# Causal attention with a softmax whose future is cleared by GpSimd: that engine's scaling, bias and additions placed in other score steps

## What is computed

```python
h = _layernorm(x) * (1 + ca) + sa                  # "x": scaled by GpSimd
att = softmax(where(causal, q @ k.T / 4, -inf))    # 16 heads, 1024 x 1024
x = x + ga * ((att @ v) @ Wp + bp)                 # bias and additions by GpSimd
h = _layernorm(x) * (1 + cb) + sb                  # "f": scaled by GpSimd
x = x + gb * ffn(h)                                # two more layers, not touched here
```

## Time and profile before

| | |
|---|---|
| median of 3 runs | 4243.48 us (4224.47 to 4245.86) |
| the profiled execution | 4219.14 us, of which the program's span is 4217.4 us |
| attention stage in it | about 0 to 1512 us, the two layers behind it 1512 to 4217 us |
| TensorE busy over the span | 3790.9 us, 90% |
| GpSimd busy over the span | 2105.5 us, 50% |

### The profile page before, as it was taken

How to read it: one execution, slowest core, us unless ns; L and a number is a source line. 1 busy time by engine, 2 the same in 40 slices (tenths; PEclk the granted TensorE clock), 3 DMA queues, 4 the chain that set the end, 5 groups by cost and what they waited for, 6 DMA issues and landing times.

```text
span 4217.4 us, 84635 instructions
## 1 busy us (share of the span) xinstructions
PE 3790.9 (90%) x31022; PEld 2881.4 (68%) x31022; DVE 3088.6 (73%) x7229; ACT 2613.4 (62%) x5759; POOL 2105.5 (50%) x2082
## 2 busy tenths in 40 slices
PE   4888898888988748999999999999999999999997
PEld 2344545444444337888888888888888888888886
DVE  5677666766677447778777787778788788888884
ACT  1455445544555426777777777777777777777774
POOL 1244444434444324555555555555565666656664
PEclk6889879978899769999999999999999999999998
DMA  5334243442443011000000000011000000000000
GB/s 130 86 66 123 59 100 74 90 121 61 100 98 77 25 61 37 17 17 19 15 20 17 17 19 16 19 35 44 29 26 22 26 23 28 26 23 25 23 24 21
DMA packets 146009, 195.72 MB, mean 46 GB/s; under 512 B 21596, under 2 KB 119608, under 8 KB 145600
## 3 DMA queue, kind: packets, MB, share of 16 engines
q1 hardware_dynamic: 145600, 190.31, 18.0%
HBM read 113.66 MB, written 67.16 MB: 43 GB/s over the span
## 4 chain that ended last, share of the span: by engine, by line
PE 24%; DVE 14%; ACT 12%; DMA 8%; issue 5%; POOL 1%; DVEq 0%; POOLq 0%; SPq 0%; ACTq 0%
PE b_bank_m L1948 10%; DMA b_hs<-b_fr 7%; PE b_bank_p L1948 5%; ACT b_e L1828 4%; DVE b_e L2176 3%; PE b_bank_et L2013 2%; DVE b_qk_rot L2145 2%; PE b_bank_t L1948 2%; ACT L1871 2%; DVE b_rot L2149 2%; PE b_bank_ot L2028 2%; PE b_bank_s L2002 1%; ACT b_e_t L1838 1%; DVE b_ag L2240 1%; ACT b_ag L1863 1%
## 5 line engine op out<-in xcount | busy, mean ns | idle before, releaser
L763 ACT ACTIVATE a_e_t<-a_ring 128x1024 f32<-128x1024 f32 (+3 forms) x768 | 610.6, 809 | 585.1 <-PE a_ring L941 580.2
L1084 DVE TENSOR_REDUCE a_mx<-a_ring 128x2 f32<-128x1024 f32 (+3 forms) x768 | 724.3, 956 | 274.7 <-PE a_ring L904 130.8
L1716 POOL TENSOR_TENSOR b_e<-b_e,b_share 128x512 f32<-128x512 f32 (+1 forms) x512 | 506.0, 991 | 802.8 <-DVE b_share L2184 802.6
L1828 ACT ACTIVATE b_e<-b_e,b_bias 128x256 f32<-128x256 f32 (+1 forms) x1024 | 494.4, 487 | 163.9 <-DVE b_bias L2176 162.8
L664 POOL TENSOR_SCALAR_AFFINE_SELECT a_e_t<-a_e_t 128x256 f32<-128x256 f32 x512 | 205.4, 407 | 720.6 <-ACT a_e_t L763 717.5
L2176 DVE CUSTOM_DVE_ANT_0 b_e<-b_bank_s,b_mask,b_inv 128x256 f32<-128x256 f32 (+1 forms) x1024 | 415.6, 460 | 33.3 <-PE b_bank_s L2002 33.3
L1701 POOL TENSOR_TENSOR b_qk_rot<-b_qk_rot,b_rot 128x512 f32<-128x512 f32 x256 | 352.4, 1386 | 129.8 <-DVE b_rot L2149 129.8
L941 PE MATMUL a_ring<-a_q_st,a_k_st 50*128 50x512 f32 (+3 forms) x1536 | 364.5, 474 | 49.5 <-DVE a_mx L1084 21.2
L1838 ACT ACTIVATE b_e_t<-b_bank_et 128x512 f32<-128x512 f32 (+1 forms) x512 | 287.3, 561 | 184.4 <-PE b_bank_et L2013 184.3
L917 PE MATMUL a_ring<-a_k_st,a_q_st 48*128 48x512 f32 (+3 forms) x1536 | 323.7, 419 | 83.5 <-ACT a_e_t L763 48.3
L958 PE MATMUL a_outp<-a_e_t,a_v_t 128*32 128x512 f32 (+3 forms) x3072 | 370.3, 557 | 30.5 <-POOL a_e_t L664 17.9
(11 more groups left out here) (235 smaller groups left out, 11117.4 us busy)
## 6 DMA issues: line engine op xcount, KB each, us to landing
a_q_st<-a_parts_q SPq DMA_DIRECT2D x192, 128.0 KB, 4.7
a_k_st<-a_parts_k SPq DMA_DIRECT2D x192, 128.0 KB, 7.5
a_parts_q<-a_qk_p SPq DMA_DIRECT2D x16, 1024.0 KB, 7.7
a_parts_k<-a_qk_p SPq DMA_DIRECT2D x16, 1024.0 KB, 9.6
b_fl<-f_rows SPq DMA_DIRECT2D x64, 256.0 KB, 4.2
a_xl<-in_L_attn_x SPq DMA_DIRECT2D x9, 1024.0 KB, 5.2
a_x<-in_L_attn_x SPq DMA_DIRECT2D x8, 1024.0 KB, 9.1
x_rows<-a_x SPq DMA_DIRECT2D x8, 1024.0 KB, 4.6
```

The costliest lines, as they stand in the source:

```text
L763: act.activation(e_t[:, step % 2, 2 * pair:2 * pair + 2, 0:cols], slot[:, :].rearrange("p (h t) -> p h t", h=2)[:, :, 0:cols], ACT.Exp).th ...
L1084: dve.reduce_max(mx[:, g % 2, :, pair, piece, t:t + 1], slot[:, :].rearrange("p (r c) -> p r c", r=2)[:, :, 0:cols], AX.X)\
L1716: pool.tensor_tensor(weights, weights, share[:, h % SPS, 2 * j:2 * j + 2].unsqueeze(2) .broadcast_to([P, 2, 2 * WIN - lo]), ALU.mult).then ...
L1828: ins = act.activation(weights, weights, ACT.Exp, scale=-1.0, bias=bias[:, h % SPS, at:at + 1], accum_out=total[:, h % SPS, at:at + 1])
```

## The change

The three tables become four, keyed by (group, step), and GpSimd's loop looks each of them up. In numbers of pieces per step:

| work | before | after |
|---|---|---|
| `modulate_f` | (1, 1) to (1, 3) one each, (1, 4) to (1, 7) two each, (1, 8) to (1, 10) one each, (1, 11) two | (1, 0) to (1, 3) one each, (1, 4) to (1, 7) three each |
| `add_bias` | (2, 8) to (2, 11) one each | (2, 5) one, (2, 6) one, (2, 7) two |
| `modulate_x` | as `modulate_f`, in group 3 | (3, 4) to (3, 6) three each, (3, 7) two, (0, 2) one, (0, 4) and (0, 5) two each |
| `add_rows` | (0, 6) two, (0, 8) two | (0, 6) two, (0, 8) one, (0, 9) one |

```diff
-PIECES_AT = (0, 1, 1, 1, 2, 2, 2, 2, 1, 1, 1, 2)
-BIAS_AT = ((2, 8), (2, 9), (2, 10), (2, 11))
-ROWS_AT = ((0, 6), (0, 8))
+F_AT = {(1, n): k for n, k in enumerate((1, 1, 1, 1, 3, 3, 3, 3))}
+X_AT = {(3, 4): 3, (3, 5): 3, (3, 6): 3, (3, 7): 2, (0, 2): 1, (0, 4): 2, (0, 5): 2}
+BIAS_AT = {(2, 5): (0,), (2, 6): (1,), (2, 7): (2, 3)}
+ROWS_AT = {(0, 6): (0, 1), (0, 8): (2,), (0, 9): (3,)}
...
+def pieces_at(plan, at):
+    place = lambda at: ((at[0] - 1) % G1, at[1])
+    before = sum(k for other, k in plan.items() if place(other) < place(at))
+    return range(before, before + plan.get(at, 0))
...
-            def add_rows(p, i):
+            def add_rows(q, i):
                 pool.wait_ge(biased.sem, biased.at(i, 1))
-                pool.wait_ge(gated.sem, gated.at(i, 2 * p + 2))
-                for q in range(2):
-                    ts = slice(4 * p + 2 * q, 4 * p + 2 * q + 2)
-                    ins = pool.tensor_tensor(x1[:, ts, :], x1[:, ts, :], f_t[:, ts, :], ALU.add)
-                ins.then_inc(x1_done.sem, 1)
+                pool.wait_ge(gated.sem, gated.at(i, 2 * (q // 2) + 2))
+                ts = slice(2 * q, 2 * q + 2)
+                ins = pool.tensor_tensor(x1[:, ts, :], x1[:, ts, :], f_t[:, ts, :], ALU.add)
+                if q % 2:
+                    ins.then_inc(x1_done.sem, 1)
```

More of the change, by code:

```diff
@@ L265 @@
 SCALED = 12
-PIECES_AT = (0, 1, 1, 1, 2, 2, 2, 2, 1, 1, 1, 2)
-BIAS_AT = ((2, 8), (2, 9), (2, 10), (2, 11))
-ROWS_AT = ((0, 6), (0, 8))
-assert sum(PIECES_AT) == SCALE_PIECES and len(PIECES_AT) == NSTEP
+F_AT = {(1, n): k for n, k in enumerate((1, 1, 1, 1, 3, 3, 3, 3))}
+X_AT = {(3, 4): 3, (3, 5): 3, (3, 6): 3, (3, 7): 2, (0, 2): 1, (0, 4): 2, (0, 5): 2}
+BIAS_AT = {(2, 5): (0,), (2, 6): (1,), (2, 7): (2, 3)}
+ROWS_AT = {(0, 6): (0, 1), (0, 8): (2,), (0, 9): (3,)}
+assert sum(F_AT.values()) == sum(X_AT.values()) == SCALE_PIECES
+def pieces_at(plan, at):
+    place = lambda at: ((at[0] - 1) % G1, at[1])
+    before = sum(k for other, k in plan.items() if place(other) < place(at))
+    return range(before, before + plan.get(at, 0))
 UNIT_AT = ((5, 1), (3, 0), (2, 0), (0, 0), (5, 0), (4, 0), (1, 0), (4, 1), (7, 1), (7, 0), (6, 1), (6, 0))
@@ L694, in program @@
                             clear_future(g, n, a)
-                        before = sum(PIECES_AT[:n])
-                        for k in range(before, before + PIECES_AT[n]):
-                            if g == 1 and i > 0:
+                        if i > 0:
+                            for k in pieces_at(F_AT, (g, n)):
                                 modulate_f(k, i - 1)
-                            if g == 3 and mode == "body":
+                        if mode != "lead":
+                            for q in BIAS_AT.get((g, n), ()):
+                                add_bias(q, i)
+                        if mode == "body":
+                            for k in pieces_at(X_AT, (g, n)):
                                 modulate_x(k, i + 2)
-                        if (g, n) in BIAS_AT:
-                            add_bias(BIAS_AT.index((g, n)), i)
-                        if mode == "body" and (g, n) in ROWS_AT:
-                            add_rows(ROWS_AT.index((g, n)), i)
+                            for q in ROWS_AT.get((g, n), ()):
+                                add_rows(q, i)
                 if mode == "closing":
-                    add_rows(0, i)
+                    for q in range(2):
+                        add_rows(q, i)
                     rows, shape = f_t[:, END:TB, :], [P, TB - END, C]
```

## The result

| | before | with the change |
|---|---|---|
| median, timed side by side | 4237.73 us (4 runs, 4224.47 to 4245.86) | 4187.27 us (4 runs, 4183.47 to 4198.07) |
| the profiled execution | 4219.1 us | 4189.7 us |
| its span, and mean granted clock | 4217.4 us, 0.938 | 4187.9 us, 0.945 |

The ratio is 0.9888, 95% interval 0.9854 to 0.9922: 1.1% faster.

The account below looks back on a forecast made before the run. In the attention stage GpSimd was not the bound, only the moment of its clearings, for which TensorE waited 17.9 us. Direct 5.2 plus clock 6.3 gave 11.5 us off the 4243.5 median: 4232 us, range 4208 to 4254.

Parts of the forecast that it names:

- The direct gain: Attention stage: shorter TensorE waits for clearings, 4.2 us from the `f` pieces and 1.0 from row additions, 5.2 in all.
- The bias: Group 2: addition runs once `x1` has landed, done 5.5 us before GpSimd is next needed; costed at nothing.
- The `x` pieces and the row additions: Groups 3 and 0: eleven `x` pieces fit with 0.9 us to spare, gaining nothing; row additions gain 1 us in all.
- The clock: Group 2: denser TensorE work avoids one clock fall in four, 6.3 us, between none and a bound of 29 us.
- the wait is not the whole cause, but it stands right where the clock falls: Group 2, wait at (2, 0): denser work there should keep the clock up more often; 6.3 us taken.
- The text named that case as one that would prove it wrong: Groups 3 or 0 changing their granted clock more than group 2 would show the prediction wrong.
- The sign that the prediction had set for its clock term: Group 2: fewer than four of the six bodies with `f` pieces lose clock.
- waits as short as those here would not matter: By the skill's rule on TensorE's idle gaps, no clock would come back in group 2, leaving the direct 5 us.
- Most of the clock comes back: Rival: three or more falls in group 2 avoided, 20 to 31 us, 4218 us in the middle; chance 0.2.

Follow-up runs that it names:

- x_only: The kernel before with only the table of the `x` pieces as changed: 4232.43 us, ratio 0.9994.
- rows_only: The kernel before with only the row additions split over (0, 8) and (0, 9): 4232.98 us, ratio 0.9991.
- f_only: The kernel before with only the table of the `f` pieces as changed: 4188.51 us, ratio 0.9888.
- bias_only: The kernel before with only the bias table as changed: 4219.42 us, ratio 0.9969.
- The filled kernels: Unread TensorE transposes added ahead of the values of (g, 0): four in group 2 of before, 0.9920; in every group of before, 0.9909, or changed, 0.9836.
- A second filling: Four more unread transposes in step (g, 0), added to the changed kernel that already had four in (g, 1): 4209.61 us, ratio 0.9945 to before.

## Why the prediction was wrong

**The direct gain.** Right in place and nearly in size. The waits on the clearings fell from 17.9 to 11.7 us, with 4.2 predicted for the waits and 5.2 in all, and at (2, 0) ScalarE's copy is what ends a wait that is left. The 0.70 us was not the wait of every body: those of before with the pair had 0.23 to 0.83 us. Another direct part was missed: seven times 1.05 us of VectorE's held instruction, an upper bound of 7.4 us.

**The bias.** "Nothing" was worked out for GpSimd's side, and that side held. SyncE issues the load of `x1` 3.6 us after the start of (2, 0), as predicted (it was 7.7), and the bias ends with 6.3 us to spare before GpSimd's next clearing waits for ScalarE:

```profile
895.19 0.43 SPq L558 DMA_DIRECT2D a_x<-in_L_attn_x  x1
...
903.54 0.73 POOL L680 TENSOR_TENSOR a_gate_bp<-a_modb,a_b_p 128x256 f32<-128x256 f32 x1 [0.86 <-DMA a_x<-in_L_attn_x]
904.35 4.98 POOL L683 TENSOR_TENSOR a_x<-a_x,a_gate_bp 128x512 f32<-128x512 f32 x4
915.64 0.41 POOL L672 TENSOR_SCALAR_AFFINE_SELECT a_e_t<-a_e_t 128x256 f32<-128x256 f32 x1 [6.32 <-ACT a_e_t L773]
```

The step that failed is that I asked only when the addition would run, not what ran beside it on VectorE in its old place. The Trainium skill has the rule on the page "SBUF — State Buffer", section on the two separate sides: VectorE's instructions with two SBUF inputs and GpSimd's share a port pair under an exclusive lock, and the one that comes second is blocked for the whole instruction. I had weighed the short form of this rule only as a thing that might slow GpSimd. The trace agrees with the page in the other direction: VectorE's instruction took 1.22 us beside an addition, in all seven bodies, and 0.17 alone.

**The `x` pieces and the row additions.** Right: x_only and rows_only are at 0.9994 and 0.9991. The run of eleven pieces ends 0.83 us before the next clearing needs GpSimd, with 0.9 predicted:

```profile
1264.27 9.66 POOL L646 TENSOR_SCALAR a_xl<-a_xl,a_x_aggr,a_x_rstd 128x256 f32<-128x256 f32 x8
1274.01 3.76 POOL L650 TENSOR_TENSOR a_xl<-a_xl,a_mod_in 128x512 f32<-128x512 f32 x3
1278.61 0.41 POOL L672 TENSOR_SCALAR_AFFINE_SELECT a_e_t<-a_e_t 128x256 f32<-128x256 f32 x1 [0.83 <-ACT a_e_t L773]
```

**The clock.** This is the term that failed, by size and by reach: 6.3 us for one fall of four avoided in group 2. Over the 95 runs of the eleven kernels without filling, time follows the mean granted clock with a correlation of -0.99, 2.8 us for each 0.001, and a scatter of 3 us around the line. The runs of the changed kernel stand at 0.944 to 0.949. A line through the 29 runs of before beside the first experiments (2.7 us per 0.001) gives 4198 us at their mean of 0.9465, and they took 4189. The line is carried past the highest clock of those 29 runs, 0.942, so what follows is an estimate: about 9 of the 50 us are direct and about 40 are clock. Most of it is what the pair does, since putting the pair back loses 38 of 47 us. The reading in the prediction was "the wait is not the whole cause, but it stands right where the clock falls", and from that I took a value near none. The runs put in its place: the clock falls in (2, 1) with or without the pair, and the pair makes the difference between a fall of 3.4 us and one of 34 or more: 15 of 15 such falls were long with it, and 3 of 16 where it was moved away. Two bodies of before had the wait and kept the clock, and I took that for evidence against a large gain; but the wait costs clock only in those bodies where the clock has just fallen. Nor was the wait alike where the clock was lost for long: it was 0.63 us in one of the two bodies and 0.23 in the other. I had also bounded the term by group 2 alone, at 29 us. The trace showed group 3 at five low lengths out of seven before, and I left them out because the direct gain hardly touches group 3. The text named that case as one that would prove it wrong, if group 3 changed more than group 2. It changed nearly as much, 24.0 against 25.6 us, and its mean granted clock rose from 0.828 to 0.942, that of group 2 from 0.856 to 0.985. With f_only, which leaves the bias, group 3 fell by 20 us too, and with bias_only, which leaves the pair, by 29. So neither move alone accounts for it, and whether a clock that is held in one group helps the next is not settled here. The sign that the prediction had set for its clock term, fewer than four of the six bodies losing clock in group 2, did come: only the fourth body lost any.

One reading of the earlier trace rows was off as well, with no weight in the sum: the first 15 slices go down to six tenths, and the last of the 40 stands at eight.

The Trainium skill's rule on falls (page "TensorE: Matmul & The Clock Gate", section on HAM oscillation) puts them down to idle gaps of TensorE between bursts. The prediction read it as saying that "waits as short as those here would not matter". The filled kernels agree with its kind, since more work of TensorE kept the low stretches short, and the traces contradict that reading: 0.63 us of idle time went with a low stretch of 34 us. Three other long ones had no wait in front of the values, so idle time is not the whole of it.

**The rivals.** "Most of the clock comes back" was the right one in kind; its 4218 was still too high by 31 us, since it counted group 2 alone. The nearest row to have used was the first body, the only one without the pair: its group 2 had kept the clock, and I called one body little.

**What stays open.** What makes the clock fall in (2, 1), in (3, 0) to (3, 3) and in the closing part in the first place was not isolated. Nor was what it is in TensorE's work behind the fall in (2, 1) that decides its length. A second filling loses in two ways: beside the line through the runs of before, its runs lie 21 us above and those with one filling 5 above, so by this estimate some 16 of the 40 us are there at equal clock and the rest is clock; why the clock is lost is open. Each kernel was profiled once, so the counts of bodies come from one execution each.

## What to carry to other kernels

Where the time of many runs follows the mean granted clock, look at what TensorE does just behind a fall of the clock, short idle times among it, and not only for the longest waits: here the pair of pieces that caused 0.2 to 0.8 us of waiting there was worth 38 us. Useless matmuls in such a wait are a quick test of whether it is the clock, and sometimes a gain that stays. And when side work is placed in GpSimd's gaps, look at what VectorE does at the same moment, not only at whether GpSimd is free.

## What the hardware did that I had not expected

- A low stretch of the clock that begins 0.2 to 1.3 us into (2, 1) lasted 3.4 us (25 times) or 34.1 to 37.5 us (18 times), and never anything between. In the kernels without filling, less than 0.1 us in the start of one group of matmuls parts the latest of the short ones (0.82 us behind the fall) from the earliest of the long ones (0.89).
- Four useless transposes, 0.66 us at full clock and 1.11 at the lower one, in each group but the lead-in's, made the changed kernel some 20 us faster; with eight it was 40 us slower than with four.
- A VectorE instruction of 128 x 8 numbers takes 0.17 us alone, 0.32 to 0.34 beside a clearing of 0.41 us and 1.22 beside an addition of 1.28 us. GpSimd's own durations did not change: its bias additions took 1.28 us with it and without.
